# Cross attention on one core: three pairs of max units a head folded into differences in the score ring

## The chip, the cores and the metric

The kernel runs on one NeuronCore of one Trainium2 chip. The core has TensorE (PE, which multiplies matrices into PSUM; PEld is its weight load), VectorE (DVE), ScalarE (ACT), GpSimd (POOL) and SyncE (SP, which here issues DMA transfers). The metric is the device time of one execution in microseconds (us). Three runs of the kernel before took 4049.95, 4050.84 and 4052.11 us, a median of 4050.84 us.

## The reference

A sequence x of 1024 rows of 128 features goes through four layers: windowed attention with a gated feed-forward, two cross attentions over a context of 6404 rows (one with a feed-forward, one with a layer norm), and a decoder layer of masked self attention, cross attention and a feed-forward. The change touches the three cross attentions. Each has 16 heads of 8 features and computes (from the second layer of the reference; the head count and the sizes of the arrays are those of the data):

```python
q = (x @ Wq + bq).reshape(b, t, NUM_HEADS, HEAD_DIM)
k = (inp @ Wk + bk).reshape(b, s, NUM_HEADS, HEAD_DIM)
v = (inp @ Wv + bv).reshape(b, s, NUM_HEADS, HEAD_DIM)
attn = jnp.einsum('bthd,bshd->bhts', q, k)
attn = jax.nn.softmax(attn / jnp.sqrt(jnp.float32(HEAD_DIM)), axis=-1)
out = jnp.einsum('bhts,bshd->bthd', attn, v).reshape(b, t, DIM)
x = x + out @ Wo + bo
```

So each head has a score for each of 1024 x 6404 pairs of query and key, a softmax over the 6404 keys, and a sum of values of 8 features.

## The kernel before, in words

The function `cross_attention` runs one layer. All three of its loops are unrolled, and each engine has its own list of instructions in a fixed order; semaphores alone tie the lists together. A head is computed in two passes.

**The max pass** finds, for each query, the largest score over the keys. It works in max units: four blocks of queries times 13 chunks of 494 keys make 52 units a head (`HEAD_UNITS`). For one unit PE runs two matmuls of 494 columns (L1707, one for the upper and one for the lower half of the queries, on different rows of the array) into one of two PSUM buffers `max_scores`, and VectorE reduces the 988 numbers to two maxima in `chunk_max` (L1859). After 52 units VectorE takes the maximum over the 13 chunks (`neg_max`, L1863), PE turns it (L1694, the "turn"), VectorE copies it out (L1855), and SP writes it as one more row behind the queries, so that the scores of the second pass come out with the maximum taken off. A unit or a turn is called an entry; before, a head has 53. PE may start entry w only when VectorE has taken entry w-2, since there are two buffers.

**The score pass** computes the scores again, the other way round (128 keys by 512 queries, one "slot", L1733), exponentiates them on ScalarE (L1838) into `probs`, a ring of 15 slots in SBUF (`RING`), and sums the values weighted by them on PE (L1760). A head has 101 slots (`HEAD_SLOTS`) and 51 value tiles (`NTILE`); a tile is two slots and four fp32 matmuls, each of which shows as two records in the trace. The PSUM tile `scores` has three banks. Score ops alternate: an op of two slots in banks 0 and 1, then an op of one slot in bank 2. Op n may start on PE when ScalarE is done with op n-2, since that one had the same banks:

```python
            def score_op(n):
                if n >= 2:
                    pe.wait_ge(exp_ready, n - 1)
```

In this text a **step** is one op of banks 0 and 1 together with the op of bank 2 behind it. Before, a step has three slots.

**The order of the work** is written out by PE's list:

```python
            for n in range(NOPS):
                score_op(n)
                for i in range(tiles_by[n - 1] if n else 0, tiles_by[n]):
                    values(i)
                for w in range(entries_through(n - 1) if n else HEAD_UNITS + LEAD, entries_through(n)):
                    max_step(w)
```

The max pass of head h+1 runs beside the score pass of head h: `entries_through` spreads 53 entries over 101 slots. `tiles_through` puts value tiles behind the one-slot ops alone, at most two each. So PE's list holds, step after step: scores of two slots, often a max unit, scores of one slot, one or two value tiles, sometimes a max unit. The first head's max pass runs by itself, beside the projection of the values; the last head's score pass runs without a max pass, in the first two layers beside the products for the next layer's keys.

Queries and keys are held as bf16 parts in 48 rows at partitions 0 to 47 and again at 64 to 111 (`head_rows`); the second half of the tile `queries` (`spare`) is free until the end of the layer. The list of slots, ops and entries comes from `slots_of_op`, `op_of_slot`, `slots_through`, `entries_through` and `max_entry`.

Of the kernel before, what the change touches and what calls it, by code (L numbers as in the profile page):

```python
# [43 lines left out]
NOPS = 2 * (H * HEAD_SLOTS // 3) + (1 if H * HEAD_SLOTS % 3 else 0)  # L44
# [6 lines left out]
NENTRY = H * (HEAD_UNITS + 1)  # L51
# [1466 lines left out]

def slots_through(op):
    return 3 * ((op + 1) // 2) + (2 if op % 2 == 0 else 0)  # L1520


def op_of_slot(g):
    return 2 * (g // 3) + (1 if g % 3 == 2 else 0)


def slots_of_op(op):
    return range(slots_through(op) - (2 if op % 2 == 0 else 1), slots_through(op))
# [6 lines left out]
def entries_through(op):  # L1535
    slots = slots_through(op)
    last = NENTRY if slots > HEAD_SLOTS * (H - 2) + HEAD_SLOTS - 9 else NENTRY - 1
    return min(last, HEAD_UNITS + LEAD + -(-(HEAD_UNITS + 1) * slots // HEAD_SLOTS))


def max_entry(w):

    if w < HEAD_UNITS:
        return 0, w
    h, v = (w - HEAD_UNITS) // (HEAD_UNITS + 1) + 1, (w - HEAD_UNITS) % (HEAD_UNITS + 1)
    if h == H or v == TURN_AFTER:
        return h - 1, None
    return h, (v if v < TURN_AFTER else v - 1)


def turn_entry(h):
    return NENTRY - 1 if h == H - 1 else HEAD_UNITS + h * (HEAD_UNITS + 1) + TURN_AFTER

# [20 lines left out]
def cross_attention(k, layer, base, qb, vb, k_parts, o_whole, wv, wo, bo, bv, tails_d, early=(), ahead=None, following=None):  # L1574
# [4 lines left out]
    with ExitStack() as ctx:  # L1579
# [8 lines left out]
        acc_s = sb("values_sum_s", [P, 2, QBLOCK])  # L1588
        sums = sb("sums", [P, N])
# [13 lines left out]
        rows_loaded = sem("rows_loaded")  # L1603
        scores_ready = sem("scores_ready")
# [82 lines left out]
        def _(pe):  # L1687
            def max_step(w):
                h, u = max_entry(w)
                if w >= 2:  # L1690
                    pe.wait_ge(max_taken, w - 1)
                if u is None:
# [4 lines left out]
                c, j = u // 4, u % 4  # L1697
                width = min(MAX_CHUNK, M - MAX_CHUNK * c)
                if u == 0 and h < 2:
# [28 lines left out]
            def score_slot(g):  # L1728
                h, x = g // HEAD_SLOTS, g % HEAD_SLOTS
                q = slice(HALF * h, HALF * (h + 1))  # L1730
                if x < 2 * (NTILE - 1):
                    rows, t = score_rows(x % 2), x // 2
                    return pe.matmul(sc[:, g % 3, :], keys(rows, h, P * t, P * (t + 1)), qb[rows, q],  # L1733
                                     start=True, stop=True)
                for half in range(2):
                    rows = score_rows(half)
                    mm = pe.matmul(sc[32 * half:32 * half + LAST_KEYS, g % 3, :], keys(rows, h, M - LAST_KEYS, M),
# [3 lines left out]
            def score_op(n):  # L1741
                if n >= 2:
                    pe.wait_ge(exp_ready, n - 1)
                for g in slots_of_op(n):
                    if g % HEAD_SLOTS == 0:
                        pe.wait_ge(rows_loaded, 32 * (g // HEAD_SLOTS + 1))
                    mm = score_slot(g)
# [61 lines left out]
        def _(act):  # L1809
# [19 lines left out]
            for n in range(NOPS):  # L1829
                if n >= 1 and tiles_by[n - 1] % NTILE == 0 and tiles_by[n - 1] > (tiles_by[n - 2] if n >= 2 else 0):  # L1830
                    take_values(tiles_by[n - 1] // NTILE - 1)
                slots = slots_of_op(n)
                act.wait_ge(scores_ready, n + 1)
                if slots[-1] >= RING:
                    freed = slots[-1] - RING
                    act.wait_ge(tile_used, NTILE * (freed // HEAD_SLOTS) + freed % HEAD_SLOTS // 2 + 1)
                a, b = slots[0], slots[-1] + 1
                act.activation(pr[:, a % RING:a % RING + b - a, :], sc[:, a % 3:a % 3 + b - a, :], ACT.Exp)\  # L1838
# [5 lines left out]
        def _(pool):  # L1844
            pool.memset(vb[:, :, :, HD:WV], 1.0).then_inc(v_ones, 1)  # L1845

        @block.vector
        def _(dve):
            def take_entry(w):
                h, u = max_entry(w)  # L1850
                dve.wait_ge(max_scores, w + 1)
                if u is None:
                    if h >= 1:
                        dve.wait_ge(rows_loaded, 32 * h)
                    dve.tensor_copy(nrow[:], mxb[0:QT, w % 2, 0, 0:P]).then_inc(max_taken, 1)  # L1855
                    return
# [33 lines left out]

            dve.memset(acc[:], 0.0).then_inc(acc_zeroed, 1)
# [229 lines left out]
```

## Time and profile before

| | |
|---|---|
| runs shown, median of 3 | 4050.84 us |
| profiled execution: time; span of its instructions | 4047.96 us; 4046.2 us |
| PE, share of the span busy | 90% |
| DVE | 84% |
| ACT | 69% |
| POOL | 6% |
| largest DMA queue (q1), share of 16 engines' span | 14.9% |

The span falls into three stages of some 1000 us, one for each cross attention, with shorter parts between them. Inside these stages PE and DVE show as busy for nearly all of the time and ACT for about 85% of it. A busy share does not tell which of them sets the pace: matmuls are pipelined and their records overlap, and so do the records of two VectorE instructions that follow each other without a gap. The pace is read from the starts of the instructions.

### The profile page before, as it was taken

To read this page: it belongs to the slowest core of one execution; us is meant where nothing else is said; L and a number is where in the kernel's file an instruction comes from. 1 tells how busy PE (TensorE), PEld (TensorE's weight loads), DVE (VectorE), ACT (ScalarE), POOL (GpSimd) and SP (SyncE) were. 2 spreads that over 40 slices of the span, in tenths; PEclk is the share of its full clock that TensorE was granted. 3 is DMA by queue.
4 is the path that set the end of the run, shared out by engine and by line. 5 is a ranking of instruction groups with operands and counts; after the bars stand their busy time and mean duration, and the time that the engine had idled before them with its cause. 6 is when DMAs were issued, how large, how long until landed. Compare 5 with 4: busy or idle time off the path is not lost. (4 is left out here: it accounts for less than half of the span.)

```text
span 4046.2 us, 85569 instructions
## 1 busy us (share of the span) xinstructions
PE 3643.4 (90%) x35190; PEld 1247.7 (31%) x35252; DVE 3396.8 (84%) x3314; ACT 2799.8 (69%) x4037; POOL 229.6 (6%) x196
## 2 busy tenths in 40 slices
PE   6796899999999969999999998599869999999997
PEld 2363222222222232222222222255422222222222
DVE  4434999999999659999999995599879999999981
ACT  0441588888888816888888886255418888888885
POOL 3000000000000000000000000244300000000000
PEclk9657799999999968999999999699859999999998
DMA  3103012111111311011011012400011101111100
GB/s 106 50 2 57 22 29 30 17 28 30 19 26 18 68 40 30 16 30 30 16 30 30 16 18 62 80 6 5 3 39 28 30 16 30 30 21 25 30 3 9
DMA packets 60005, 118.34 MB, mean 29 GB/s; under 512 B 11618, under 2 KB 51746, under 8 KB 54370
## 3 DMA queue, kind: packets, MB, share of 16 engines
q1 hardware_dynamic: 56196, 110.19, 14.9%
q8 instruction: 258, 4.23, 0.4%
q10 hardware_dynamic: 3456, 3.15, 0.3%
q14 instruction: 95, 0.78, 0.1%
HBM read 84.95 MB, written 28.26 MB: 28 GB/s over the span
## 5 line engine op out<-in xcount | busy, mean ns | idle before, releaser
L1859 DVE TENSOR_REDUCE chunk_max<-max_scores 128x2 f32<-128x988 f32 (+1 forms) x2496 | 2787.0, 1177 | 122.0 <-PE max_scores L1707 82.9
L1838 ACT ACTIVATE probs<-scores 128x512 f32<-128x512 f32 (+1 forms) x3231 | 2453.2, 808 | 459.1 <-PE scores L1733 434.2
L1760 PE MATMUL values_sum<-probs,values 128*9 128x256 f32 x19584 | 1367.7, 382 | 0.0
L1733 PE MATMUL scores<-queries,key_ring 49*128 49x512 bf16 x4800 | 1226.6, 384 | 44.5 <-ACT probs L1838 12.1
L1707 PE MATMUL max_scores<-key_ring,queries 48*128 48x494 bf16 (+1 forms) x4992 | 979.7, 391 | 161.0 <-DVE chunk_max L1859 105.5
L1760 PEld LDWEIGHTS values_sum<-probs,values 128*9 128x9 f32 x19584 | 374.7, 89 | 758.0 <-issue 570.4
L1707 PEld LDWEIGHTS max_scores<-key_ring,queries 48*128 48x128 bf16 x4992 | 240.4, 94 | 853.0 <-DVE chunk_max L1859 528.9
L1733 PEld LDWEIGHTS scores<-queries,key_ring 49*128 49x128 bf16 x4800 | 305.2, 94 | 636.3 <-ACT probs L1838 546.3
L1392 ACT ACTIVATE probs<-scores 128x512 f32<-128x512 f32 x256 | 138.5, 592 | 106.0 <-PE scores L1344 106.0
L1811 ACT ACTIVATE values<-scores 128x512 f32<-128x512 f32 (+2 forms) x45 | 25.1, 565 | 209.3 <-PE scores L1717 195.6
L1418 DVE TENSOR_REDUCE chunk_max<-max_scores 128x1024 f32 (+1 forms) x128 | 154.9, 1213 | 8.8 <-PE max_scores L1300 8.7
L1409 POOL TENSOR_TENSOR probs_low<-probs 128x512 bf16<-128x512 f32 (+1 forms) x128 | 135.8, 1061 | 180.6 <-ACT probs L1392 180.6
L1441 DVE TENSOR_TENSOR probs_low<-probs 128x512 bf16<-128x512 f32 x128 | 142.4, 1113 | 1.2 <-ACT probs L1392 1.2
L1300 PE MATMUL max_scores<-mask_query_key,ident_b 128*128 128x512 bf16 x256 | 99.7, 390 | 21.2 <-DMA key_ring<-k_self 20.5
L1344 PE MATMUL scores<-mask_key_query,ident_b 128*128 128x512 bf16 x256 | 96.8, 378 | 4.4 <-ACT queries L1380 0.9
L1298 PE MATMUL max_scores<-key_ring,queries 128*128 (+1 forms) x242 | 94.3, 390 | 3.8 <-DVE chunk_max L1418 3.4
L1342 PE MATMUL scores<-queries,key_ring 128*128 (+1 forms) x208 | 78.9, 380 | 0.0
L879 ACT ACTIVATE probs<-probs,neg_max 128x96 f32<-128x96 f32 x128 | 46.0, 363 | 47.6 <-DVE neg_max L831 47.6
L1314 PE MATMUL values_sum<-values,probs 128*128 (+1 forms) x1024 | 67.9, 174 | 11.2 <-POOL probs_low L1409 8.9
L1314 PEld LDWEIGHTS values_sum<-values,probs 128*128 128x128 bf16 x1024 | 62.7, 97 | 31.9 <-issue 17.0
L1845 POOL MEMSET values<- 128x816 f32 x3 | 4.7, 1556 | 1183.0 <-POOLq L127 1183.0
L1717 PE MATMUL scores<-squares,context 128*128 128x128 f32 x288 | 70.4, 421 | 0.0
(205 smaller groups left out, 1637.4 us busy)
## 6 DMA issues: line engine op xcount, KB each, us to landing
key_ring<-k_parts SPq DMA_DIRECT2D x96, 300.2 KB
key_ring<-k_parts SPq DMA_DIRECT2D x96, 200.1 KB
key_ring<-k_parts SPq DMA_DIRECT2D x96, 100.1 KB
k_parts<-queries SPq DMA_DIRECT2D x72, 128.0 KB, 2.4
o_whole<-values_sum_s SPq DMA_DIRECT2D x45, 128.0 KB, 8.0
queries<-q_rows SPq DMA_DIRECT2D x8, 672.0 KB, 9.5
k_parts<-k_part SPq DMA_DIRECT2D x36, 128.0 KB, 2.4
context<-in_ctx_t SPq DMA_DIRECT2D x1, 3202.0 KB, 17.2
```

The lines of the kernel that those rows point to most:

```text
L1300: mm = pe.matmul(out, k.ident_b[:], mask[0][:, bass.ds(i * cw + t * nk, cw)], start=False, stop=True)
L1314: pe.matmul(out, high(half, a, a + P), v, start=(first_tile and t == 0), stop=False, skip_group_check=True)
L1344: mm = pe.matmul(sc_bank[c][0:tk, :], k.ident_b[:], mask[1][:, bass.ds((i * TPI + j) * N + c * HALF, HALF)], start=False, stop=True)
L1392: act.activation(pr[0:tk, 2 * j + c, :], sc_bank[c][0:tk, :], ACT.Exp).then_inc(exp_ready, 1)
L1409: pool.tensor_tensor(pr_low[0:tk, 2 * j, 0:mine], pr[0:tk, 2 * j, 0:mine], high(2 * j, 0, mine), ALU.subtract).then_inc(low_pool, 1)
L1418: dve.tensor_reduce(mx[:, bass.ds(slot * (ni * QT) + i * QT + 2 * u, 2)], mx_bank[u % 2][:, :, 0:cw], AX.X, ALU.max).then_inc(max_taken, 1)
L1441: dve.tensor_tensor(pr_low[0:tk, half, 0:HALF], pr[0:tk, half, 0:HALF], high(half, 0, HALF), ALU.subtract).then_inc(low_dve, 1)
L1707: mm = pe.matmul(mxb[:, w % 2, half, 0:width], qb[rows, HALF * h + P * j:HALF * h + P * (j + 1)], keys(rows, h, MAX_CHUNK * c, MAX_CHUNK * ...
L1733: return pe.matmul(sc[:, g % 3, :], keys(rows, h, P * t, P * (t + 1)), qb[rows, q], start=True, stop=True)
L1760: mm = pe.matmul(acc[32 * b:32 * b + WV, 0:QBLOCK], vb[rows, h, t, :], pr[rows, slot, QBLOCK * (b % 2):QBLOCK * (b % 2 + 1)], start=(t == ...
L1838: act.activation(pr[:, a % RING:a % RING + b - a, :], sc[:, a % 3:a % 3 + b - a, :], ACT.Exp)\
L1859: dve.tensor_reduce(mx[:, h % 2, c, :, j], mxb[:, w % 2, :, 0:width], AX.X, ALU.max)\
```

## The change

Two of the 13 chunks of a head (numbers 10 and 11) are taken together for three of the four query blocks, in all heads but the first. Since max(a, b) = a + relu(b - a), PE computes the difference of the two chunks' scores in PSUM, ScalarE applies relu and writes the result to a new SBUF tile `gain`, PE computes the scores of chunk 10 as before into `max_scores`, and VectorE adds `gain` to them and takes the maximum in one instruction for each half of the queries. Six max units become three "fold" entries a head, so a head has 50 entries instead of 53.

The difference is four matmuls of 494 columns: two with the queries on chunk 11, and two with the negated queries on chunk 10, accumulated into the same banks. They go into banks 0 and 1 of `scores`, and so take the place of a two-slot op in the alternation. The negated queries are made by GpSimd in `spare`, once a layer. The list of score ops is now made by `score_ops`, which also splits a two-slot op where it would run over the end of the ring of 15.

```diff
+FOLD_A, FOLD_B = 10, 11
+FOLD_AT = (12, 26, 40)
+NFOLD = len(FOLD_AT)
+HEAD_ENTRIES = HEAD_UNITS - NFOLD + 1
+NENTRY = HEAD_UNITS + (H - 1) * HEAD_ENTRIES + 1
...
+def fold_due(f):
+
+    return HEAD_SLOTS * (fold_entry(f) - HEAD_UNITS - LEAD) // HEAD_ENTRIES - 8
+
+
+def score_ops():
+
+    ops, g, f, pair = [], 0, 0, True
+    while g < H * HEAD_SLOTS:
+        if not pair:
+            ops.append(("exp", g, 1, 2))
+            g += 1
+        elif f < NFOLD * (H - 1) and fold_due(f) <= g:
+            ops.append(("difference", f, 0, 0))
+            f += 1
+        else:
+            count = 2 if g + 1 < H * HEAD_SLOTS and g % RING != RING - 1 else 1
+            ops.append(("exp", g, count, 0))
+            g += count
+        pair = not pair
+    return ops
...
-    return min(last, HEAD_UNITS + LEAD + -(-(HEAD_UNITS + 1) * slots // HEAD_SLOTS))
+    return min(last, HEAD_UNITS + LEAD + -(-HEAD_ENTRIES * slots // HEAD_SLOTS))
...
+            def difference(f):
+                h, j = f // NFOLD + 1, f % NFOLD
+                a, b = MAX_CHUNK * FOLD_A, MAX_CHUNK * FOLD_B
+                if f == 0:
+                    pe.wait_ge(negated, 2)
+                for half in range(2):
+                    rows, q = head_rows(half), slice(HALF * h + P * j, HALF * h + P * (j + 1))
+                    pe.matmul(sc[:, half, 0:MAX_CHUNK], qb[rows, q], keys(rows, h, b, b + MAX_CHUNK), start=True, stop=False)
+                for half in range(2):
+                    rows, q = head_rows(half), slice(HALF * h + P * j, HALF * h + P * (j + 1))
+                    mm = pe.matmul(sc[:, half, 0:MAX_CHUNK], spare[rows, q], keys(rows, h, a, a + MAX_CHUNK),
+                                   start=False, stop=True)
+                return mm
...
+                kind, a, count, bank = OPS[n]
                 act.wait_ge(scores_ready, n + 1)
...
+                if kind == "difference":
+                    if a >= 1:
+                        act.wait_ge(max_taken, fold_entry(a - 1) + 1)
+                    act.activation(gain[:], sc[:, 0:2, 0:MAX_CHUNK], ACT.Relu).then_inc(exp_ready, 1)
+                    continue
...
+            pool.wait_ge(k.rest_rows[layer], 32)
+            for half in range(2):
+                pool.wait_ge(negated if half else v_ones, 1)
+                pool.tensor_scalar(spare[head_rows(half), :], qb[head_rows(half), 0:H * HALF], -1.0, None, ALU.mult)\
+                    .then_inc(negated, 1)
...
+                if kind == "fold":
+                    dve.wait_ge(exp_ready, OP_OF_FOLD[NFOLD * (h - 1) + u] + 1)
+                    for half in range(2):
+                        fold = dve.tensor_tensor_reduce(
+                            out=gain[:, half, :], in0=mxb[:, w % 2, half, 0:MAX_CHUNK], in1=gain[:, half, :], scale=1.0,
+                            scalar=-BIG, op0=ALU.add, op1=ALU.max, accum_out=mx[:, h % 2, FOLD_A, half, u:u + 1])
+                    fold.then_inc(max_taken, 1)
```

How the lists move. On PE, in the middle of a head's score pass, the list before runs (L1733 scores, L1707 max unit, L1760 value tiles):

```order
L1733 MATMUL scores<-queries,key_ring 128x512 x2
L1707 MATMUL max_scores<-key_ring,queries 128x494 x2
L1733 MATMUL scores<-queries,key_ring 128x512
L1760 MATMUL values_sum<-probs,values 9x256 x4
L1733 MATMUL scores<-queries,key_ring 128x512 x2
L1707 MATMUL max_scores<-key_ring,queries 128x494 x2
L1733 MATMUL scores<-queries,key_ring 128x512
L1760 MATMUL values_sum<-probs,values 9x256 x8
L1707 MATMUL max_scores<-key_ring,queries 128x494 x2
```

and the list after, at a difference (L1787 and L1790 are its two passes, L1799 scores, L1759 max unit, L1830 value tiles):

```order
L1799 MATMUL scores<-queries,key_ring 128x512 x2
L1759 MATMUL max_scores<-key_ring,queries 128x494 x2
L1799 MATMUL scores<-queries,key_ring 128x512
L1830 MATMUL values_sum<-probs,values 9x256 x8
L1787 MATMUL scores<-key_ring,queries 128x494 x2
L1790 MATMUL scores<-key_ring,queries 128x494 x2
L1799 MATMUL scores<-queries,key_ring 128x512
L1830 MATMUL values_sum<-probs,values 9x256 x4
L1759 MATMUL max_scores<-key_ring,queries 128x494 x2
L1799 MATMUL scores<-queries,key_ring 128x512 x2
```

The two passes of the difference stand where two slots of scores and a max unit stood; the one-slot op and its value tiles behind them are as they were.

On ACT, at the end of a head, the list after runs (L1907 relu of a difference, L1912 exponentials, L1897 the copy of a head's sums):

```order
L1907 ACTIVATE gain<-scores 128x988
L1912 ACTIVATE probs<-scores 128x512
L1897 ACTIVATE values_sum_s<-values_sum 128x256
L1912 ACTIVATE probs<-scores 128x1024
L1912 ACTIVATE probs<-scores 128x512
L1912 ACTIVATE probs<-scores 128x1024
L1912 ACTIVATE probs<-scores 128x512 x3
```

Before, exponentials of 1024 and of 512 alternate without exception there; now one of 988 has come in, and in the row with x3 the middle one is a two-slot op cut to one slot at the end of the ring.

On DVE, over one head, the list after runs (L1948 max units, L1941 fold):

```order
L1936 CAST neg_max_rows<-max_scores 8x128
L1948 TENSOR_REDUCE chunk_max<-max_scores 128x2 x9
L1941 ISA gain,chunk_max<-max_scores,gain 128x494
L1941 ISA chunk_max 128x1
L1941 ISA gain,chunk_max<-max_scores,gain 128x494
L1941 ISA chunk_max 128x1
L1948 TENSOR_REDUCE chunk_max<-max_scores 128x2 x13
```

A fold is four instructions: for each half of the queries the addition with its running maximum, and a short one that writes the maximum out. Before, this stretch was one row of max units.

## Rows read from the trace of the kernel before

**Rows 1.** Busy time by engine over one head, from its neg_max to the next.
```profile
1043.50:1103.90 60.40, 58.57 (x620) 16.96 (x622) 58.56 (x55) 51.45 (x70) 0.00 (x0) 1.00 0.18 25
```

**Rows 2.** Groups by line and shape: busy us, mean ns, idle before and releasers.
```profile
L1859 DVE TENSOR_REDUCE chunk_max<-max_scores 128x2 f32<-128x988 f32 x2304 | 2579.3, 1180 | 116.4 <-PE max_scores L1707 80.6
L1838 ACT ACTIVATE probs<-scores 128x1024 f32<-128x1024 f32 x1617 | 1656.5, 1024 | 447.2 <-PE scores L1733 425.5 <-PE scores L1737 9.9
L1838 ACT ACTIVATE probs<-scores 128x512 f32<-128x512 f32 x1614 | 955.6, 592 | 11.9 <-PE scores L1733 8.7
```

**Rows 3.** VectorE timeline: start us, length us, first max pass, then a later head.
```profile
372.02 4.47 DVE L1859 TENSOR_REDUCE chunk_max<-max_scores 128x2 f32<-128x988 f32 x4 [0.67 <-PE max_scores L1707]
...
1043.47 0.34 DVE L1863 TENSOR_REDUCE neg_max<-chunk_max 128x8 bf16<-128x104 f32 x1
...
1049.36 54.49 DVE L1859 TENSOR_REDUCE chunk_max<-max_scores 128x2 f32<-128x988 f32 x48 [0.30 <-PE max_scores L1707]
1103.88 0.35 DVE L1863 TENSOR_REDUCE neg_max<-chunk_max 128x8 bf16<-128x104 f32 x1
```

**Rows 4.** ScalarE timeline, a middle head, then the last head's score pass.
```profile
1006.03 3.02 ACT L1838 ACTIVATE probs<-scores 128x1024 f32<-128x1024 f32 x4 [0.45 <-PE scores L1733]
1009.55 3.02 ACT L1838 ACTIVATE probs<-scores 128x1024 f32<-128x1024 f32 x4 [0.49 <-PE scores L1733]
...
1020.52 3.02 ACT L1838 ACTIVATE probs<-scores 128x1024 f32<-128x1024 f32 x4 [0.38 <-PE scores L1733]
1023.92 3.02 ACT L1838 ACTIVATE probs<-scores 128x1024 f32<-128x1024 f32 x4 [0.38 <-PE scores L1733]
...
3959.05 3.02 ACT L1838 ACTIVATE probs<-scores 128x1024 f32<-128x1024 f32 x4 [0.28 <-PE scores L1733]
3962.34 3.02 ACT L1838 ACTIVATE probs<-scores 128x1024 f32<-128x1024 f32 x4 [0.28 <-PE scores L1733]
```

**Rows 5.** Timeline of PE and ScalarE over two steps, 908.67 to 912.83 us.
```profile
908.67 0.38 PE L1707 MATMUL max_scores<-key_ring,queries 48*128 48x494 bf16 x1
908.89 0.38 PE L1733 MATMUL scores<-queries,key_ring 49*128 49x512 bf16 x2
...
909.31 3.02 ACT L1838 ACTIVATE probs<-scores 128x1024 f32<-128x1024 f32 x4 [0.45 <-PE scores L1733]
...
909.64 0.62 PE L1760 MATMUL values_sum<-probs,values 128*9 128x256 f32 x8
910.39 0.10 PEld L1733 LDWEIGHTS scores<-queries,key_ring 49*128 49x128 bf16 x2 [0.63 <-ACT probs L1838]
...
910.88 0.09 PEld L1733 LDWEIGHTS scores<-queries,key_ring 49*128 49x128 bf16 x1 [0.38 <-ACT probs L1838]
...
911.20 1.05 PE L1760 MATMUL values_sum<-probs,values 128*9 128x256 f32 x16
...
912.18 0.38 PE L1707 MATMUL max_scores<-key_ring,queries 48*128 48x494 bf16 x2
...
912.40 0.38 PE L1733 MATMUL scores<-queries,key_ring 49*128 49x512 bf16 x2
...
912.83 1.02 ACT L1838 ACTIVATE probs<-scores 128x1024 f32<-128x1024 f32 x1 [0.49 <-PE scores L1733]
```

**Rows 6.** VectorE groups near to a fold's two instructions.
```profile
L1882 DVE TENSOR_TENSOR queries<-max_scores,queries 128x512 f32<-128x512 f32 x12 | 8.3, 692 | 0.4
L1884 DVE SCALAR_TENSOR_TENSOR queries<-max_scores,vectors,queries 128x512 f32<-128x512 f32 x12 | 9.0, 751 | 0.4
L1177 DVE TENSOR_TENSOR k_part<-k_rest,k_part 128x512 bf16<-128x512 f32 x2 | 3.1, 1567 | 0.1
L254 DVE SCALAR_TENSOR_TENSOR pooled<-pooled,vectors 128x1 f32<-128x1 f32 x1 | 0.2, 219 | 0.0
L416 DVE MEMSET eps<- 128x1 f32 x1 | 0.1, 59 | 0.0
```

**Rows 7.** GpSimd group near to the negation.
```profile
L2005 POOL TENSOR_SCALAR mask_query_key<-mask_bytes_query_key 128x8192 bf16<-128x8192 uint8 x1 | 7.1, 7069 | 0.1
```

More of the change, by code:

```diff
@@ L1516, in score_rows, with head_entries, fold_entry @@
     return slice(64 * half, 64 * half + KROWS + 1)
+def head_entries():
+    entries = [("unit", 4 * c + j) for c in range(NCHUNK) for j in range(4)
+               if not (c in (FOLD_A, FOLD_B) and j < NFOLD)]
+    entries.insert(TURN_AFTER, ("turn", None))
+    for j, at in enumerate(FOLD_AT):
+        entries.insert(at, ("fold", j))
+    return entries
+ENTRIES = head_entries()
+def fold_entry(f):
+    return HEAD_UNITS + f // NFOLD * HEAD_ENTRIES + FOLD_AT[f % NFOLD]
+def fold_due(f):
[15 more added lines that the diff above has]
+    return ops
+OPS = score_ops()
+NOPS = len(OPS)
+SLOTS_THROUGH = list(itertools.accumulate(count for _, _, count, _ in OPS))
+OP_OF_SLOT = [n for n, (_, _, count, _) in enumerate(OPS) for _ in range(count)]
+OP_OF_FOLD = [n for n, op in enumerate(OPS) if op[0] == "difference"]
 def slots_through(op):
-    return 3 * ((op + 1) // 2) + (2 if op % 2 == 0 else 0)
+    return SLOTS_THROUGH[op]
 def op_of_slot(g):
-    return 2 * (g // 3) + (1 if g % 3 == 2 else 0)
-def slots_of_op(op):
-    return range(slots_through(op) - (2 if op % 2 == 0 else 1), slots_through(op))
+    return OP_OF_SLOT[g]
 def tiles_in(slots):
@@ L1696, in max_step @@
                     return
-                c, j = u // 4, u % 4
+                c, j = (FOLD_A, u) if kind == "fold" else (u // 4, u % 4)
                 width = min(MAX_CHUNK, M - MAX_CHUNK * c)
-                if u == 0 and h < 2:
+                if kind == "fold":
+                    pass
+                elif u == 0 and h < 2:
                     pe.wait_ge(k.first_keys[layer], 16 * (2 * NPART * 2 + (2 if layer == 0 else 0)))
@@ L1743, in score_op @@
                     pe.wait_ge(exp_ready, n - 1)
-                for g in slots_of_op(n):
+                kind, first, count, bank = OPS[n]
+                if kind == "difference":
+                    difference(first).then_inc(scores_ready, 1)
+                    return
+                for g in range(first, first + count):
                     if g % HEAD_SLOTS == 0:
                         pe.wait_ge(rows_loaded, 32 * (g // HEAD_SLOTS + 1))
-                    mm = score_slot(g)
+                    mm = score_slot(g, bank + g - first)
                 mm.then_inc(scores_ready, 1)
@@ L1849, in take_entry @@
             def take_entry(w):
-                h, u = max_entry(w)
+                h, kind, u = max_entry(w)
                 dve.wait_ge(max_scores, w + 1)
-                if u is None:
+                if kind == "turn":
                     if h >= 1:
                         dve.wait_ge(rows_loaded, 32 * h)
+                    else:
+                        dve.memset(mx[:, 0, FOLD_B, :, 0:NFOLD], -BIG)
                     dve.tensor_copy(nrow[:], mxb[0:QT, w % 2, 0, 0:P]).then_inc(max_taken, 1)
+                    return
+                if kind == "fold":
+                    dve.wait_ge(exp_ready, OP_OF_FOLD[NFOLD * (h - 1) + u] + 1)
[4 more added lines that the diff above has]
+                    fold.then_inc(max_taken, 1)
                     return
```

38 lines of the change are left out of this document (20 added, 18 removed).

## The prediction

> **What bounds the kernel now.** I read the page first, then the heads one by one. A head of a cross attention, from its neg_max to the next, takes 60.4 us (1043.47 to 1103.88) [rows 3]; three layers have 15 such heads each, so 45 heads are two thirds of the span, and the change works in these alone. In one head PE shows 58.57 us busy of 60.40, DVE 58.56 and ACT 51.45, at a granted clock of 1.00 [rows 1]. By that, PE and DVE are both full, and the change would pay, as it takes work from DVE. So the next thing to read is the distance between starts.
>
> Max units that find their data ready follow each other every (4.47 - 1.18) / 3 = 1.097 us, or 1.10 [rows 2, 3]; the 1.18 of one is partly covered by the next. In the middle of a head 48 units take (54.49 - 1.18) / 47 = 1.13 us each [rows 3]. So DVE needs 52 x 1.10 + 0.34 for neg_max = 57.5 us, and a short copy for the turn, of the 60.4: it has gaps, and all that the trace names behind them is PE's max matmuls [rows 2]. DVE is nearly the bound, not the bound.
>
> The pace is seen on ACT. Its exponentials of 1024 and 512 columns follow each other without a gap for two steps (3.02 us, four instructions), then it idles 0.38 to 0.49 us for scores, and starts again after 3.51 us (1006.03, 1009.55) or 3.40 us (1020.52, 1023.92) [rows 4]. The timeline of PE shows why. In the step with one value tile (909.64) the next two-slot op waits for ACT (910.39) and ACT never idles: 1.51 us. In the step with two tiles the one-slot op waits for ACT until 910.88, then come two tiles (911.20), a max unit (912.18), and only at 912.40 the next two slots, which ACT gets at 912.83: 2.00 us, half a microsecond of it idle on ACT [rows 5]. No instruction of DVE is in that chain. The last head's score pass, which has no max units beside it, still takes 3.30 us for two steps (3959.05, 3962.34) [rows 4]. So a loop of PE's order and ACT's two-op ring sets 3.30 to 3.51 us for two steps, and three max units there need DVE for 3 x 1.097 = 3.29 us.
>
> As a check: before, a head has 101 / 3 = 33.67 steps. By the code's lists (averages of heads 2 to 13, here and below) 17.33 have two tiles and 16.33 one. At 2.00 and 1.51 that is 59.3 us; 1.0 us is left, for the turn and for those double steps that hold four max units instead of three.
>
> **What the change does, part by part.** *VectorE.* Six units of 1.10 us become three folds. The trace has no fold. Nearest are one addition of a PSUM and an SBUF tile (512 columns, 0.692 us; with a third operand 0.751), and for the short instruction one column (0.059 for a memset, 0.219 for an arithmetic one) [rows 6]. So a fold costs between 2 x 0.75 = 1.50 and 2 x 0.97 = 1.94 us; I take 1.6, near the addition it is. That saves 0.6 of 2.2 us a pair, 1.8 us a head, 135 pairs in all. DVE then needs 46 x 1.10 + 4.8 + 0.34 = 55.7 us a head.
>
> The Trainium skill (VectorE: DVE Perf Modes, The TRN2 errata) prices an fp32 addition at (N + 151) / 0.96 ns: 691 for 512 columns, and the trace agrees with 692 [rows 6]; for 494 the estimate is 672. The same page (Two Vector instructions with no wait between them) counts an accumulator output as a second instruction, an accumulator read, for which no row here has a time. By these a fold would be 1.34 us and the reads; the sum would not move, since DVE isn't what it goes by.
>
> *Steps.* This is the cost that I think decides. A difference is no slot, but it takes the place of a two-slot op, so its step has one slot instead of three. And since the slots no longer come in threes, the ring of 15 ends inside a two-slot op, which is cut to one: that step has two. A layer's list of score ops grows from 1077 to 1167, or by 45 steps, 3 a head: 36.67 steps, of which 30.67 are ordinary, 3 have a difference and 3 are cut.
>
> *Ordinary steps.* 13.08 have two tiles, 17.58 one or none: 13.08 x 2.00 + 17.58 x 1.51 = 52.7 us. The price stays, as the order inside them stays: a max unit behind two tiles, none behind one, which is the pattern of 3.51 us [rows 5].
>
> *Steps with a difference.* On PE the four matmuls take 2 x 0.22 us (two on different rows of the array cost the 0.22 between 908.67 and 908.89), where two slots and a max unit stood [rows 5]; on ACT relu over 988 columns stands for an exponential of 1024 at 1.02 [rows 2]. I price it as an ordinary step: 2 with two tiles and 1 with one, 5.5 us. From below, 0.21 less where no max unit stands behind two tiles (the 3.30 against the 3.51 [rows 4]), a third of a step; from above 0.22 more each, since relu starts only behind the second pass.
>
> *Cut steps.* 0.92 with two tiles, 2.08 with one or none. ACT needs two exponentials of 512 at 1.51 - 1.02 = 0.49 us each. With two tiles PE needs one slot 0.22, a max unit 0.22, one slot with what lies behind it 0.32 (910.88 to 911.20) and the tiles 0.98 (911.20 to 912.18), in all 1.74 [rows 5]. So 0.98 to 1.51 us, and 1.74 to 2.00. I take 1.2 and 1.75: 4.1 us, within 3.6 and 5.0.
>
> *The rest.* The four-unit double steps are gone; turn and folds keep 0.4 us (0 to 2.2: the 1.0 of before, and 0.4 a fold for entries queued behind it on PE). A fold waits for relu as well; the difference is placed some eight slots ahead, over 4 us, so nothing waits there; behind a fold that did wait stand DVE's next units, and PE's entry after next. Relu waits for the fold before it, which is a dozen entries back. The negation on GpSimd is two instructions of 8192 columns, 7.07 us each by the nearest row [rows 7]; it lies beside the first head's max pass of at least 52 x 1.10 = 57 us, which covers it four times over. If that cover failed, PE's list would stand still in the third step of the first head, and ACT behind it. Relu asks for no new table load in ACT's list. SP's transfers keep their waits and their order.
>
> *Sum.* 52.7 + 5.5 + 4.1 + 0.4 = 62.7 us a head against 60.4: 2.3 to 2.4 more. 45 heads: +107 us. The profiled execution took 4047.96 us, 1.8 more than its span; so 4155 there, and 4158 against the median of the runs shown, which is 2.9 above it. DVE would then idle some 7 us a head: it is freed, and nothing comes of it.
>
> With all low ends a head is 52.4 + 5.4 + 3.6 + 0 = 61.4, +1.0, so 4096. With all high ends it is 52.7 + 6.2 + 5.0 + 2.2 = 66.1, which all at once is unlikely; half way from my values to there is +4.0, 4231.
>
> **The rivals.** *VectorE decides (the other side).* If a head follows DVE's work, it loses 1.8 us: 45 x 1.8 = 81, so 3970. For it: DVE's busy share, and the four-unit double steps, where PE does wait for DVE. Against: the 0.03 us gaps between units [rows 3], and 3.30 us for two steps with no units at all. It decides only if two steps can be done in less than three units need, 3.29 us; in the last head's rows they aren't. The Trainium skill (Perfetto Trace Analysis, Identifying the Most-Contended Engine) would optimise the engine of highest occupancy first, and that favours this rival; the starts in the trace don't. Chance 0.07.
>
> *ScalarE alone prices the new steps.* If PE hides all else, difference steps cost 1.51 and cut ones 0.98: 52.4 + 4.5 + 2.9 + 0.4 = 60.2 us, no change, 4051. Against: two value tiles behind a one-slot op delay ACT in every row. Chance 0.06.
>
> *The fold is slow.* The slowest addition in the trace, both inputs in SBUF, took 1.567 us [rows 6]. A fold would be 2 x (1.57 + 0.22) = 3.6 us; PE may be two entries ahead, 2 x 3.51 / 3 = 2.34 us, so each fold holds up the list by 1.2: 135 x 1.2 = 162 on top, 4320. Against: one input is in PSUM, as in the rows at 0.69. Chance 0.07.
>
> **How the numbers follow.** The forecast, longer steps, has 0.80 and its time is 4158. Its own range is 4090 to 4230, which holds 0.77 of its 0.80; with some of the neighbouring cases (the end of no change, a mildly slow fold) that makes 0.8, so it is the range. About 0.2% (8 us) is what can be told from no change here. Faster by more: 0.07, the VectorE case. Within: 0.05, nearly all the ScalarE case. Slower by more: 0.88.
>
> **What would show it.** In the profile after: a head period near 62.7 us; DVE's gaps growing to several us a head, ended by PE's max matmuls, and its busy share falling; ACT's two ordinary steps still 3.51 us apart; a step from relu to the next two-slot exponential at 1.5 or 2.0 us; a cut step at 1.2 to 1.8; fold instructions near 0.7 us. I am wrong if ordinary double steps shrink below 3.4 us now that DVE has room, or if steps with a difference or a cut take about 1.2 us.

## The result, and the profile after

The changed kernel takes 4149.66 us (median of 4 runs, 4146.06 to 4152.99) against 4050.39 for the kernel before in the same comparison: a ratio of 1.0257, 95% interval 1.0242 to 1.0271. It is slower by 99 us; forecast were 107.

The page of the kernel after: busy time of each engine with its share of the span (4144.2 us), then five groups (line, engine, operation, count | busy us, mean ns | idle us before, and who ended it).

```profile
PE 3705.4 (89%) x35522; PEld 1258.3 (30%) x35522; DVE 3280.1 (79%) x3590; ACT 2930.7 (71%) x4307; POOL 355.0 (9%) x202
...
L1948 DVE TENSOR_REDUCE chunk_max<-max_scores 128x2 f32<-128x988 f32 (+1 forms) x2226 | 2514.8, 1179 | 317.3 <-PE max_scores L1759 279.8
L1912 ACT ACTIVATE probs<-scores 128x512 f32<-128x512 f32 (+1 forms) x3366 | 2467.5, 783 | 378.7 <-PE scores L1799 364.8
...
L1941 DVE CUSTOM_DVE_ANT_0 gain<-max_scores,gain 128x494 f32<-128x494 f32 x270 | 169.9, 666 | 16.5 <-PE max_scores L1759 12.9
...
L1907 ACT ACTIVATE gain<-scores 128x988 f32<-128x988 f32 x135 | 134.2, 994 | 51.8 <-PE scores L1790 51.8
...
L1923 POOL TENSOR_SCALAR queries<-queries 48x8192 bf16<-48x8192 bf16 x6 | 125.4, 20897 | 21.0 <-DMA queries<-q_rows 20.8
```

VectorE's share fell from 84% to 79%, and its idle time before max units rose from 122.0 us (116.4 for those of 988 columns alone [rows 2]) to 317.3, of which 279.8 were ended by PE's max matmuls: it was freed, and it waits.

VectorE's timeline over one head (start us, length us): the neg_max at both ends, and one fold between.

```profile
1064.08 0.35 DVE L1952 TENSOR_REDUCE neg_max<-chunk_max 128x8 bf16<-128x104 f32 x1
...
1079.80 0.66 DVE L1941 CUSTOM_DVE_ANT_0 gain<-max_scores,gain 128x494 f32<-128x494 f32 x1
1080.38 0.08 DVE L1941 DVE_READ_ACCUMULATOR2_ANT chunk_max<- 128x1 f32 x1
1080.38 0.67 DVE L1941 CUSTOM_DVE_ANT_0 gain<-max_scores,gain 128x494 f32<-128x494 f32 x1
1080.98 0.08 DVE L1941 DVE_READ_ACCUMULATOR2_ANT chunk_max<- 128x1 f32 x1
...
1126.35 0.34 DVE L1952 TENSOR_REDUCE neg_max<-chunk_max 128x8 bf16<-128x104 f32 x1
```

This head takes 62.27 us against 60.41 [rows 3]. The fold takes 1.26 us from the first start to the last end.

Over that head (columns as in [rows 1]) VectorE is busy 55.91 us, 2.65 less than before, and PE 59.16, 0.59 more:

```profile
1064.10:1126.30 62.20, 59.16 (x627) 16.96 (x621) 55.91 (x60) 54.20 (x75) 0.00 (x0) 1.00 0.17 24
```

ScalarE's timeline, first ordinary steps, then a difference:

```profile
870.89 3.02 ACT L1912 ACTIVATE probs<-scores 128x1024 f32<-128x1024 f32 x4 [0.49 <-PE scores L1799]
874.39 3.02 ACT L1912 ACTIVATE probs<-scores 128x1024 f32<-128x1024 f32 x4 [0.48 <-PE scores L1799]
...
886.50 0.99 ACT L1907 ACTIVATE gain<-scores 128x988 f32<-128x988 f32 x1 [0.24 <-PE scores L1790]
887.39 0.59 ACT L1912 ACTIVATE probs<-scores 128x512 f32<-128x512 f32 x1
887.87 0.39 ACT L1897 ACTIVATE values_sum_s<-values_sum 128x256 f32<-128x256 f32 x1
888.16 4.10 ACT L1912 ACTIVATE probs<-scores 128x1024 f32<-128x1024 f32 x6
```

Two ordinary steps are still 3.50 us apart (870.89, 874.39), as in [rows 4]. The step that the relu opens takes 888.16 - 886.50 = 1.66 us and carries one slot.

From the starts of ScalarE's instructions (averages of heads 2 to 13 of the three layers, here and below) a head before is 60.35 us, all in ordinary steps. After it is 53.27 in ordinary steps, 5.10 with a difference and 4.17 in cut ones, 62.54 in all. The 2.19 more, times 45 heads, are 98 us of the measured 99.

### The profile page after: what moved, and what is told of

It reads as the page before. It is cut to its first block and busy times, and to the rows that moved or that the text cites. A ratio compares the mean times of both kernels' runs of the same rounds, so it can differ in the third digit from the quotient of the medians.

```text
span 4144.2 us, 87134 instructions
## 1 busy us (share of the span) xinstructions
PE 3705.4 (89%) x35522; PEld 1258.3 (30%) x35522; DVE 3280.1 (79%) x3590; ACT 2930.7 (71%) x4307; POOL 355.0 (9%) x202
## 5 line engine op out<-in xcount | busy, mean ns | idle before, releaser
L1948 DVE TENSOR_REDUCE chunk_max<-max_scores 128x2 f32<-128x988 f32 (+1 forms) x2226 | 2514.8, 1179 | 317.3 <-PE max_scores L1759 279.8
L1912 ACT ACTIVATE probs<-scores 128x512 f32<-128x512 f32 (+1 forms) x3366 | 2467.5, 783 | 378.7 <-PE scores L1799 364.8
L1830 PE MATMUL values_sum<-probs,values 128*9 128x256 f32 x19584 | 1380.4, 382 | 0.1
L1799 PE MATMUL scores<-queries,key_ring 49*128 49x512 bf16 x4800 | 1259.8, 385 | 128.2 <-ACT probs L1912 74.1
L1759 PE MATMUL max_scores<-key_ring,queries 48*128 48x494 bf16 (+1 forms) x4722 | 940.6, 391 | 101.4 <-DVE chunk_max L1948 61.7
L1799 PEld LDWEIGHTS scores<-queries,key_ring 49*128 49x128 bf16 x4800 | 316.6, 94 | 910.7 <-ACT probs L1912 775.7
L1830 PEld LDWEIGHTS values_sum<-probs,values 128*9 128x9 f32 x19584 | 368.7, 89 | 688.0 <-issue 527.0
L1759 PEld LDWEIGHTS max_scores<-key_ring,queries 48*128 48x128 bf16 x4722 | 228.8, 94 | 664.4 <-issue 384.8
L1941 DVE CUSTOM_DVE_ANT_0 gain<-max_scores,gain 128x494 f32<-128x494 f32 x270 | 169.9, 666 | 16.5 <-PE max_scores L1759 12.9
L1907 ACT ACTIVATE gain<-scores 128x988 f32<-128x988 f32 x135 | 134.2, 994 | 51.8 <-PE scores L1790 51.8
L1923 POOL TENSOR_SCALAR queries<-queries 48x8192 bf16<-48x8192 bf16 x6 | 125.4, 20897 | 21.0 <-DMA queries<-q_rows 20.8
L1346 PE MATMUL scores<-queries,key_ring 128*128 (+1 forms) x256 | 97.1, 379 | 0.7 <-ACT queries L1384 0.7
```

The source lines that it names most:

```text
L1759: mm = pe.matmul(mxb[:, w % 2, half, 0:width], qb[rows, HALF * h + P * j:HALF * h + P * (j + 1)], keys(rows, h, MAX_CHUNK * c, MAX_CHUNK * ...
L1799: return pe.matmul(sc[:, bank, :], keys(rows, h, P * t, P * (t + 1)), qb[rows, q], start=True, stop=True)
L1830: mm = pe.matmul(acc[32 * b:32 * b + WV, 0:QBLOCK], vb[rows, h, t, :], pr[rows, slot, QBLOCK * (b % 2):QBLOCK * (b % 2 + 1)], start=(t == ...
L1907: act.activation(gain[:], sc[:, 0:2, 0:MAX_CHUNK], ACT.Relu).then_inc(exp_ready, 1)
L1912: act.activation(pr[:, a % RING:a % RING + count, :], sc[:, bank:bank + count, :], ACT.Exp)\
L1923: pool.tensor_scalar(spare[head_rows(half), :], qb[head_rows(half), 0:H * HALF], -1.0, None, ALU.mult)\
```

## The experiments

**The halves apart.** First the folds without differences, then the differences without folds.

```diff
...
-        elif f < NFOLD * (H - 1) and fold_due(f) <= g:
+        elif f < 0:
...
-                            out=gain[:, half, :], in0=mxb[:, w % 2, half, 0:MAX_CHUNK], in1=gain[:, half, :], scale=1.0,
+                            out=folded[:, half, :], in0=mxb[:, w % 2, half, 0:MAX_CHUNK], in1=gain[:, 0, :], scale=1.0,
...
+            dve.memset(gain[:], 0.0)
...
```

> The changed kernel without the differences, the relu and the negation: the ring has its old 33.67 steps a head, VectorE takes 50 entries a head with the folds adding a tile of zeros (so chunk 11 of three query blocks is left out of the maximum). Theory (the steps of the score ring set the time): 17.33 steps at 2.00 and 16.33 at 1.52 us and 0.3 us for the turn make 59.8 us a head against 60.4, 45 heads: some 25 us less than before, 4025 us (4010 to 4035). Rival (VectorE sets the time): a fold showed as 1.2 us in the changed kernel where two units took 2.2, so 3 us a head less, 45 x 3 = 135 us less, 3915 us.

3995.76 us, ratio 0.9872 (0.9856 to 0.9888). One head of it (columns as in [rows 1]):

```profile
1092.20:1151.20 59.00, 56.92 (x615) 16.25 (x609) 55.91 (x60) 51.15 (x69) 0.00 (x0) 1.00 0.17 26
```

Its group of max units, on the page:

```profile
L1943 DVE TENSOR_REDUCE chunk_max<-max_scores 128x2 f32<-128x988 f32 (+1 forms) x2226 | 2513.5, 1179 | 174.8 <-PE max_scores L1759 117.7
```

Faster by 54 us. VectorE loses the same 2.65 us of work a head as in the whole change (55.91 against 58.56 [rows 1]), but the head loses 1.2 and the rest turns into waits for PE. Both the 25 us of the theory and the 135 of the rival miss it. A fold also leaves PE one max unit to compute in place of two, so this run relieves PE a little as well; the last experiment separates the two.

```diff
...
-HEAD_ENTRIES = HEAD_UNITS - NFOLD + 1
+HEAD_ENTRIES = HEAD_UNITS + 1
...
-               if not (c in (FOLD_A, FOLD_B) and j < NFOLD)]
+               ]
...
-    for j, at in enumerate(FOLD_AT):
-        entries.insert(at, ("fold", j))
...
```

> The changed kernel with the differences and their relu in the ring, but no folds: VectorE reduces all 52 units of every head, nothing reads the relu's result, nothing is left out of the output. Theory (steps): the head of the changed kernel, 62.5 us, and the three entries more, at 0.2 to 0.3 us each: 63.1 to 63.5, so 4175 to 4195 us. Rival (it is the fold, its instructions on VectorE or its wait for relu, that made the changed kernel slower): without folds the time goes back to that of before, 4050 to 4070 us.

4210.13 us, ratio 1.0403 (1.0383 to 1.0422): slower by 160, without a single fold. That is more than the 4175 to 4195 of the theory, and the rival (the time of before) falls. A head is 63.8 us. The halves nearly add up: -54 + 160 = +106, against +99 for both. What costs is the differences in the score ring. From the folds alone (59.19 us a head) to the whole change (62.54), ordinary steps lose 5.92 us, and the steps with a difference (5.10) and the cut ones (4.17) come in: 3.35 more a head, 151 of the 154 us between these two kernels.

**No cuts.** A spare sixteenth slot takes what runs over the end of the ring.

```diff
...
-            count = 2 if g + 1 < H * HEAD_SLOTS and g % RING != RING - 1 else 1
+            count = 2 if g + 1 < H * HEAD_SLOTS else 1
...
+PLACE = [RING if i == 1 and (a + i) % RING == 0 else (a + i) % RING
+         for kind, a, count, _ in OPS if kind == "exp" for i in range(count)]
...
-        pr = sb("probs", [P, RING, HALF])
+        pr = sb("probs", [P, RING + 1, HALF])
...
```

> The changed kernel with one spare slot behind the ring, into which the second slot of a two-slot op goes where it would run over the end, so that no op is cut: 35.67 steps a head instead of 36.67. (Two small tiles of the layer's end move into the tile of the relu to make room.) Theory (steps): the three cut steps cost 4.17 us a head in the trace of the changed kernel; their six slots now are two ordinary steps at 1.755, 3.5 us. So 0.65 us a head less, 29 us: 4120 us (4110 to 4130). Rival (the differences' own work is the whole cost, a cut is free): no change, 4150 us.

4138.66 us, ratio 1.0223 (1.0205 to 1.0241): 11 us better than the change, where the theory expected some 29. Three cut steps at 4.17 us are gone, but two ordinary steps came instead, and ordinary steps rose by 3.97: I had priced them at an average, 1.755 each. The value tiles of the cut steps had to go somewhere: 1.92 more ordinary steps have two tiles. Steps are to be priced at the margin: two steps at 1.5 us, and 0.5 for each of the 1.92 that took over a second tile, are 3.96.

**Value tiles elsewhere.** In the kernel before, one tile behind every op; then the tiles behind two-slot ops instead of one-slot ones, before and after.

```diff
...
-        if op % 2 == 1 and op >= 3:
+        if op >= 3:
...
-            for _ in range(2):
+            for _ in range(1):
...
```

> The kernel before with one value tile at most behind each score op, two-slot ops included, instead of up to two behind one-slot ops. Theory A (ScalarE's wait behind two tiles is the whole of what a step costs above 1.51 us): double steps fall to 3.3 us at most, VectorE's 57.5 us a head is next, 2.9 us a head less: 3920 us. Theory B (PE's list itself needs nearly the whole double step: two slots 0.22, one slot 0.22, a unit 0.22, a tile 0.43 and some 0.22 for each change between tiles and scores): three runs of tiles instead of two in a double step, 3.46 us against 3.53, so 4000 to 4050 us.

4129.23 us, ratio 1.0203 (1.0183 to 1.0223). Slower by 80; both theories had it faster or equal. PE's and ScalarE's timeline of one step:

```profile
900.12 0.38 PE L1733 MATMUL scores<-queries,key_ring 49*128 49x512 bf16 x1
...
900.42 0.62 PE L1760 MATMUL values_sum<-probs,values 128*9 128x256 f32 x8
...
900.98 0.38 PE L1707 MATMUL max_scores<-key_ring,queries 48*128 48x494 bf16 x2
...
901.20 0.38 PE L1733 MATMUL scores<-queries,key_ring 49*128 49x512 bf16 x2
...
901.51 0.62 PE L1760 MATMUL values_sum<-probs,values 128*9 128x256 f32 x8
901.62 2.58 ACT L1838 ACTIVATE probs<-scores 128x1024 f32<-128x1024 f32 x3 [0.49 <-PE scores L1733]
...
902.06 0.38 PE L1707 MATMUL max_scores<-key_ring,queries 48*128 48x494 bf16 x2
...
902.28 0.81 PE L1733 MATMUL scores<-queries,key_ring 49*128 49x512 bf16 x3
```

No wait of PE's matmuls shows from 900.12 to 902.28, and the step is 2.16 us. One tile by itself takes 0.56 (900.42 to 900.98), two in a row 0.98 [rows 5]: the second costs 0.42, so that 0.14 belong to the run; and a scores op in front of tiles takes 0.30 where a max unit in front of scores takes 0.22. By these few rows, each run of tiles costs about 0.2 us on PE beside its tiles, an estimate. One tile behind each op makes 51 runs a head of 33.67, 17.3 x 0.2 = 3.5 us more on PE, of which some 1.9 came through (62.3 against 60.35).

```diff
...
-        if op % 2 == 1 and op >= 3:
+        if op % 2 == 0 and op >= 4:
...
```

> The kernel before with its runs of value tiles behind the two-slot ops instead of the one-slot ops, the same number and length of runs. Theory B (PE's list needs 3.24 us for a double step, and waits 0.2 for ScalarE in the step with one tile): 3.45 us a double step against 3.53, 3990 to 4030 us. Theory A (the wait of ScalarE's next two-slot op behind two tiles is all that a step costs above 1.51 us, and a one-slot op has that time to spare): VectorE's 57.5 us a head are next, 3920 to 3940 us. Rival (the place of the tiles is not what sets the step): 4050 us.

> The changed kernel with its runs of value tiles behind the ops of banks 0 and 1, differences among them. Theory B: the gain of a double step is that of the kernel before with tiles moved, 0.06 to 0.1 us, 4090 to 4120 us. Theory A: VectorE's 54.5 us a head leave the steps at 1.51, 36.67 of them 55.4 us, 3830 us. Rival (the place of the tiles is not what sets the step): 4150 us.

Before: 4111.46 us, ratio 1.0165 (1.0146 to 1.0183), a miss for all three. After: 4136.64, ratio 1.0225 (1.0206 to 1.0244), 13 better than the change, though the two intervals touch. The number of runs of tiles stays here, so their price doesn't explain it. In the kernel before, a step with two tiles still takes 1.92 to 2.00, but one with one tile now 1.65 to 1.73 in place of 1.53 to 1.56. In one such step PE waits first for VectorE and then for ScalarE:

```profile
902.41 0.10 PEld L1707 LDWEIGHTS max_scores<-key_ring,queries 48*128 48x128 bf16 x2 [0.26 <-DVE chunk_max L1859]
...
902.95 0.10 PEld L1733 LDWEIGHTS scores<-queries,key_ring 49*128 49x128 bf16 x2 [0.44 <-ACT probs L1838]
```

Why it costs 67 us before and nothing after, where it may even help, stays open.

**Half the value columns.** To take work off PE alone, each value tile works on half of its columns, before and after.

```diff
...
-                    mm = pe.matmul(acc[32 * b:32 * b + WV, 0:QBLOCK], vb[rows, h, t, :],
-                                   pr[rows, slot, QBLOCK * (b % 2):QBLOCK * (b % 2 + 1)],
+                    mm = pe.matmul(acc[32 * b:32 * b + WV, 0:QBLOCK // 2], vb[rows, h, t, :],
+                                   pr[rows, slot, QBLOCK * (b % 2):QBLOCK * (b % 2) + QBLOCK // 2],
...
```

> The kernel before with value tiles over half of the queries only (128 of 256 columns a matmul, the other half of the sums stays at a constant), so a tile takes PE half as long and the run of two tiles some 0.43 us less; nothing else is changed. Theory (a step lasts ScalarE's 1.51 us, and half a microsecond more where PE's run of two tiles stands between): a step with two tiles falls from 2.00 to 1.57, a head to 17.33 x 1.57 + 16.33 x 1.51 = 51.9 us on that side, below VectorE's 57.5, which now sets the time: 57.5 to 58.3 us a head, with the faster last heads 3905 to 3950 us in all. Rival (VectorE sets the time before already): hardly any change, above 4020 us.

> The changed kernel with the same cut: value tiles over half of the queries only. Theory: ordinary steps 13.08 x 1.57 + 17.58 x 1.51, differences 3 x 1.5, cut steps 3.8, so 55.7 us a head beside VectorE's 54.5: 55.7 to 56.5 us, and 3840 to 3890 us in all, which is 50 to 80 us faster than the kernel before with the same cut: the change would pay where the score ring has room. Rival (a difference costs its time whatever the ring's state): some 100 us slower than the kernel before with the same cut.

4863.88 us (4650.71 to 4881.65) and 4508.78 (4268.03 to 4802.18). TensorE was granted its lower clock for much of these runs (a mean of 0.587 and 0.723 in their traces, against 0.93 for the change), so their times say nothing on the theories. Where the second ran at full clock its heads took 56.9 to 57.7 us, below the 62.5 of the change. VectorE was busy for 57.12 of 60 us there (1068 to 1128), so this doesn't tell whether PE's chain or VectorE set them. These runs were also to show whether a difference costs less where the ring has room; that stays untested. The last section returns to the clock.

**Max units elsewhere.** The last three runs leave the tiles where they are and let max units (and folds) follow one tile rather than two, up to two entries early. In the kernel before, 3.0 of the 17.33 steps with two tiles still have a unit behind them, with folds none.

```diff
...
+        early = 0 if op % 2 == 1 and tiles[op] - tiles[op - 1] == 2 else 2
+        if total < min(last, due + early):
+            total += 1
...
```

> The kernel before, its max units alone put elsewhere in PE's list: the units behind one-slot ops now follow those with one value tile (16.33 a head) and no longer those with two (from 9.67 down to 3.0). Nothing else changes; the number of instructions is the same. Theory (a step with two tiles is a chain on PE, and each instruction in it lengthens the step): a step with two tiles and no unit behind them costs 1.75 to 1.89 us in place of 2.00, a step with one tile and a unit still about 1.55. A head is then 14.33 x 1.85 + 16.33 x 1.55 + 3.0 x 2.0 = 57.8 us against 60.4: 3930 to 3990 us. Rival (VectorE is so near to full that a better order of PE's list gives nothing): 4035 to 4060 us. A second rival (ACT or PE pay for the unit in the one-tile step what the two-tile step saves): 4050 us, with one-tile steps at 1.7.

> The changed kernel with the same other places of its max units and folds: none behind two value tiles. By the theory about 12 steps a head lose 0.2 us each, a head falls from 62.5 to 60.0 or 60.5: 4035 to 4065 us. VectorE needs 55 us a head here and is no bound. If VectorE's time or the number of instructions sets the pace, 4140 to 4150 as without the edit.

> The folds alone (they add zeros; no differences, so chunk 11 is left out of the maximum for three query blocks), with no max unit behind two value tiles. It gives the room on VectorE to a shorter chain on PE. Theory: 17.33 x 1.79 + 16.33 x 1.55 = 56.3 us a head against 59.1, and VectorE needs about 55: 3865 to 3900 us. Rival (PE's list is simply full): 3985 to 4000, as the folds alone.

| | its own order | units behind one tile |
|---|---|---|
| the kernel before | 4050.39 | 4043.34, ratio 0.9992 (0.9981 to 1.0004) |
| folds alone | 3995.76, ratio 0.9872 (0.9856 to 0.9888) | 3923.46, ratio 0.9695 (0.9666 to 0.9725) |
| folds and differences (the change) | 4149.66, ratio 1.0257 (1.0242 to 1.0271) | 4087.99, ratio 1.0096 (1.0068 to 1.0123) |

(The medians stand beside kernels before of 4048 to 4050 us.) In the kernel before, the order is worth nothing: the theory fails there and the first rival holds. In stretches two steps are 3.40 us apart in place of 3.51, but others are longer, and the head stays at 60.3. VectorE's timeline says why (36 units in one row):

```profile
998.98 40.56 DVE L1881 TENSOR_REDUCE chunk_max<-max_scores 128x2 f32<-128x988 f32 x36
1039.58 0.34 DVE L1885 TENSOR_REDUCE neg_max<-chunk_max 128x8 bf16<-128x104 f32 x1
...
1099.56 0.34 DVE L1885 TENSOR_REDUCE neg_max<-chunk_max 128x8 bf16<-128x104 f32 x1
```

Units follow each other every (40.56 - 1.18) / 35 = 1.125 us there, and 52 of these are 58.5 of the 60 us. With folds, VectorE has room and the same order is worth 72 us (folds alone, 3995.76 to 3923.46); in the change 62. Both gain less than the theory had: 3865 to 3900 and 4035 to 4065 were expected. ScalarE's steps with folds alone and the new order, 3.40 apart:

```profile
883.49 3.02 ACT L1934 ACTIVATE probs<-scores 128x1024 f32<-128x1024 f32 x4 [0.38 <-PE scores L1821]
886.89 3.02 ACT L1934 ACTIVATE probs<-scores 128x1024 f32<-128x1024 f32 x4 [0.38 <-PE scores L1821]
```

That it is VectorE's room, and not the three max units fewer on PE, shows in steps with the same entries on PE in both kernels. In the new order, a step with two tiles and no unit behind them takes 2.00 us with all units and 1.89 with folds; one with one tile and a unit 1.563 and 1.525. 14.33 and 16.33 of these make 2.2 of the 2.7 us between the two heads (60.34 and 57.64). PE's waits for VectorE between 700 and 1250 us (us, times, longest; idle time of the weight load, partly beside running matmuls), with all units and with folds (2.2 us more there are waits for folds):

```profile
PEld max_scores L1729 <- DVE chunk_max L1881: 94.2, 216, 1.0
...
PEld max_scores L1781 <- DVE chunk_max L1965: 41.1, 143, 0.5
```

So the two bounds lie close together: with its chain shortened, the kernel before still needs 60.3 us a head for VectorE, and with VectorE relieved its chain of PE and ScalarE needs 59.2. Folds alone win 54 us, the order alone nothing (4043 against 4048 in the same comparison), both together 125. The differences cost 154 us on top of the folds in one order and 165 in the other. The run at 3923.46 us beats both kernels, but it takes no maximum over chunk 11 in three query blocks, and so is no replacement. No version with the full maximum was found that beats the kernel before.

## Why the prediction was right

Its mechanism held: three more steps a head in the score ring cost more than VectorE's relief gave back. The sum came within 0.2 us a head (62.7 forecast, 62.54 measured), with a little luck: difference steps priced 0.4 too high in all outweigh the 0.2 that the other terms were too low. The terms one by one:

- **Ordinary steps.** 52.7 us forecast, 53.27 measured: two tiles at 2.00 us, as priced, one or none at 1.545 in place of 1.51. They did not shrink below 3.4 us for two, which would have refuted it.
- **Difference steps.** 5.5 forecast, 5.10 measured: 1.78 with two tiles, 1.53 with one. With two tiles they take 1.81 where a max unit stands behind the tiles (1.67 of the 2 a head) and 1.66 where none does, so a unit shows as 0.15 in place of 0.21, but the level lies 0.2 below the 2.00 of an ordinary step; why was not separated. Relu does wait for the second pass: the idle time of its group, 51.8 us in 135, is all ended by L1790.
- **Cut steps.** 4.1 forecast, 4.17 measured. But without cuts only 11 us come back: the sum was right, and what a cut costs by itself is little, since its step also carries tiles. One of the forecast's own signs of being wrong, cut steps of about 1.2 us, was badly set: it had priced those with one tile or none at 1.2 itself, and they took 1.20 and 1.08 (all three together 1.39 on average).
- **The rest.** 0.4 forecast. The steps as counted here fill the whole head, so this term lies within the ordinary ones: together 53.1 forecast, 53.27 measured. The wait of folds for relu never showed: of the 16.5 us before fold instructions, 12.9 are waits for PE.
- **The fold** was mis-sized, on the safe side: 1.2 to 1.26 us, below my range of 1.50 to 1.94. I rounded the addition up and let the two halves end one after the other; the next starts after 0.58 (1079.80, 1080.38), before the first has ended. The Trainium skill (VectorE: DVE Perf Modes, The TRN2 errata) gave an estimate of 672 ns for the addition; the trace has 666. It names the accumulator's read as an instruction of its own (Two Vector instructions with no wait between them), and here that takes 83 ns (22.4 us in 270), nearly all of it beside the next instruction. The group by shape:

```profile
L1941 DVE DVE_READ_ACCUMULATOR2_ANT chunk_max<- 128x1 f32 x270 | 22.4, 83 | 0.0
```

- **The negation** was mis-sized by three: 20.9 us each for 7.07. The cover I named was the right thing to check: both halves end at 375.98 + 41.88 = 417.86, and the first scores start at 441.75. GpSimd's timeline in the first layer:

```profile
375.98 41.88 POOL L1923 TENSOR_SCALAR queries<-queries 48x8192 bf16<-48x8192 bf16 x2 [7.32 <-DMA queries<-q_rows]
```

PE's timeline there, at the first scores:

```profile
441.75 0.61 PE L1799 MATMUL scores<-queries,key_ring 49*128 49x512 bf16 x2 [0.24 <-DMA queries<-neg_max_rows]
```

- **"Nearly the bound, not the bound"** was wrong on VectorE. I argued from gaps of 0.03 us, from 3.51 us for two steps, and from 3.30 in the last head's rows, which is level with the 3.29 that three units need. I also left out PE's waits for VectorE, which stood in the trace before: between 700 and 1250 us the weight loads of max units idled 82.8 us for it, 198 times, against 34.8 us with folds alone. Shortening PE's chain alone changes nothing (60.3 us a head), and relieving VectorE alone brings the head to 59.2, the 59.3 that I had summed for the chain. So what I had left over, 1.0 us for the turn and for steps with four units, was mostly VectorE. Relieving it was worth 54 us in the kernel's order and about 120 in the other (4043 to 3923). The forecast came out right all the same, since with three more steps a head the chain is the longer of the two; a sum for the folds alone by the same reading came out too small (25 us expected, 54 measured).

The rivals: *VectorE decides* falls for the change (it idles 317 us and the head grew), though it is part of what the folds alone gain. The rule of the Trainium skill that stood beside it (Perfetto Trace Analysis, Identifying the Most-Contended Engine) would be half right here: its engine was a bound of the kernel before (60.3 us a head), with a second one right behind (59.2). *The fold is slow* falls by the 666 ns and by the differences alone, slower still without folds. *ScalarE alone prices the new steps* falls with two tiles at 1.78 in difference steps and 1.85 in cut ones, where it had 1.51 and 0.98.

## What to carry to other kernels

Where two engines are both near full, ask of a change that moves work between them which one has a spare slot in its order, not which one has idle time: three differences a head are 1.3 us of PE's matmuls (3 x 2 x 0.22) and 3.0 of ScalarE's time (3 x 0.99), both of them with idle time in each head, and in a ring of alternating buffers they cost 3.4 (154 us over 45 heads). Price an added step at the margin, with the work that it takes along from other steps. When two bounds lie close together, a single edit shows little; try it together with the edit that lowers the other bound before judging it (54 and 0 us apart, 125 together).

## What the runs showed of the hardware

**Less work on TensorE, and a slower kernel.** With half of the value columns the granted clock was at 0.50, the lower level (1.2 GHz), for hundreds of microseconds. Two stretches of the kernel before with half the columns (length, busy us of PE, PEld, DVE, ACT and POOL, granted clock, DMA share, GB/s):

```profile
900.00:1200.00 300.00, 300.00 (x2306) 81.63 (x2305) 225.91 (x203) 192.62 (x256) 0.00 (x0) 0.50 0.13 20
1200.00:1500.00 300.00, 300.00 (x2302) 81.43 (x2298) 225.89 (x203) 192.32 (x256) 0.00 (x0) 0.50 0.13 20
```

and the fall inside a head of the kernel after with half the columns:

```profile
1128.00:1132.00 4.00, 3.18 (x51) 1.34 (x47) 3.67 (x6) 3.61 (x5) 0.00 (x0) 1.00 0.00 0
1132.00:1136.00 4.00, 3.46 (x47) 1.18 (x41) 3.92 (x4) 3.63 (x6) 0.00 (x0) 1.00 0.17 39
1136.00:1140.00 4.00, 3.86 (x49) 1.13 (x47) 2.86 (x3) 3.80 (x7) 0.00 (x0) 1.00 1.05 131
1140.00:1144.00 4.00, 3.79 (x29) 0.94 (x27) 3.04 (x4) 2.99 (x5) 0.00 (x0) 0.62 0.82 120
1144.00:1148.00 4.00, 4.00 (x36) 1.15 (x28) 2.87 (x6) 2.34 (x5) 0.00 (x0) 0.50 0.39 65
```

PE had gaps at full clock, was busy for 3.71 to 4.00 of every 4.00 us at the lower one, and stayed at 0.50 until about 1192 us; that head took 73.5 us, the one before it 57.7. What ended the full clock was not tested.

**The same in small, in the kernel after.** In one head of two of the layers PE idled for 0.69 us waiting for ScalarE (824.62), and just after it the granted clock was 0.56 over 3.9 us. The wait by itself doesn't explain the fall: 57 such waits of 0.69 us stand in the trace, and the clock fell behind two of them. PE's timeline at the wait:

```profile
824.62 0.39 PE L1799 MATMUL scores<-queries,key_ring 49*128 49x512 bf16 x1 [0.69 <-ACT probs L1912]
```

The stretches before and after it (columns as above):

```profile
823.50:825.40 1.90, 1.21 (x7) 0.20 (x4) 1.90 (x2) 1.86 (x3) 0.00 (x0) 1.00 0.72 145
825.40:829.30 3.90, 3.90 (x32) 0.86 (x33) 2.48 (x3) 2.24 (x4) 0.00 (x0) 0.56 0.66 103
```

These two heads took 64.56 us, and the same head of the third layer, where the clock stayed at 1.00, 62.98. That is 3 us in all and not what made the change slower.

**GpSimd by shape.** 48 partitions of 8192 bf16 values times -1 took 20.9 us, where 128 partitions of 8192 bytes into bf16 had taken 7.07 [rows 7]. Which of the type, the operation or the partitions makes it, no run here tells.
